# Attention of an adaLN block: one add of the softmax sum moved from VectorE to TensorE

## The reference

```python
scores = jnp.einsum('bhqd,bhkd->bhqk', q, k) / math.sqrt(hd)
causal = jnp.tril(jnp.ones((l, l), bool))
scores = jnp.where(causal, scores, -jnp.inf)
att = jax.nn.softmax(scores, axis=-1)
out = jnp.einsum('bhqk,bhkd->bhqd', att, v)
out = out.transpose(0, 2, 1, 3).reshape(b, l, d)
return out @ Wo.T + bo
```

## Time and profile before

| what | value |
|---|---|
| median of 3 timed runs | 2920.46 us (2919.89 to 2921.38) |
| profiled execution | 2918.9 us |
| its span, first to last instruction | 2917.2 us |
| TensorE busy (matmuls) | 2764.7 us, 95% |
| VectorE busy | 1578.7 us, 54% |
| ScalarE busy | 1058.9 us, 36% |
| GpSimd busy | 1281.3 us, 44% |
| mean granted TensorE clock | 0.979 of full speed |

### The profile page before, as it was taken

One profiled execution on the slowest core, in us unless ns is written; L12 is line 12 of the kernel. 1 busy time (PEld: TensorE's weight loads), 2 busy tenths in 40 slices (PEclk: granted clock), 3 DMA queues, 4 the chain that ended last, 5 costly groups with the idle time before them and its releaser, 6 DMA issues. The chain is left out here.

```text
span 2917.2 us, 41697 instructions
## 1 busy us (share of the span) xinstructions
PE 2764.7 (95%) x16180; PEld 2009.6 (69%) x16180; DVE 1578.7 (54%) x3165; ACT 1058.9 (36%) x1446; POOL 1281.3 (44%) x672
## 2 busy tenths in 40 slices
PE   4999999999999999889999999999999958999997
PEld 2888888888888888645555555555555527888886
DVE  4232223222323122267887777777777726777775
ACT  1322322122113111245666656556565631112121
POOL 2322332242225111267777777777777741212120
PEclk8999999999999999899999999999999979999998
DMA  7444343334335644365555555555555244544541
GB/s 250 161 159 160 140 181 134 140 116 173 116 115 169 213 164 168 127 138 121 117 117 118 122 127 127 118 126 127 128 121 117 67 146 142 148 148 138 166 130 58
DMA packets 153996, 404.85 MB, mean 139 GB/s; under 512 B 21820, under 2 KB 57076, under 8 KB 152776
## 3 DMA queue, kind: packets, MB, share of 16 engines
q1 hardware_dynamic: 123480, 292.05, 29.4%
q10 hardware_dynamic: 30320, 110.15, 17.7%
HBM read 270.41 MB, written 131.20 MB: 138 GB/s over the span
## 5 line engine op out<-in xcount | busy, mean ns | idle before, releaser
L1093 ACT ACTIVATE prob<-ps_s 128x1024 f32<-128x1024 f32 (+3 forms) x768 | 597.2, 810 | 407.2 <-PE ps_s L1231 390.4
L787 PE MATMUL ps_u<-h_hi,w_hi 128*128 128x512 f32 x1536 | 612.5, 399 | 2.0 <-POOL h_lo L555 2.0
L787 PE MATMUL ps_u<-h_lo,w_hi 128*128 128x512 f32 x1536 | 601.3, 391 | 0.0
L787 PE MATMUL ps_u<-h_hi,w_lo 128*128 128x512 f32 x1536 | 600.0, 391 | 0.0
L1049 POOL TENSOR_TENSOR added<-added,prob 128x2048 f32<-128x2048 f32 (+1 forms) x128 | 550.5, 4301 | 4.6
L549 POOL TENSOR_TENSOR w_lo<-w_raw,w_hi 128x1024 fp32r<-128x1024 f32 x93 | 222.6, 2393 | 473.1 <-ACT w_hi L617 473.1
L678 DVE SCALAR_TENSOR_TENSOR qk_lo<-ps_u,bias_col,qk_hi 128x512 fp32r<-128x512 f32 x128 | 96.0, 750 | 578.9 <-ACT qk_hi L593 578.9
L1135 DVE TENSOR_REDUCE part_high<-ps_r 128x1 f32<-128x512 f32 x496 | 330.6, 686 | 88.1 <-PE ps_r L1201 88.1
L1131 DVE CUSTOM_DVE_ANT_0 ps_r<-ps_r,row_mask 128x384 f32<-128x384 f32 (+1 forms) x500 | 312.5, 630 | 108.7 <-PE ps_r L1201 107.6
L1201 PE MATMUL ps_r<-k_st,q_st 96*128 96x512 f32 (+1 forms) x1008 | 330.9, 386 | 16.8 <-DMA v_sb<-v_tok 9.0
L787 PEld LDWEIGHTS ps_u<-h_lo,w_hi 128*128 128x128 f32 x1536 | 288.7, 188 | 61.6
(11 more groups left out here) (197 smaller groups left out, 3429.6 us busy)
## 6 DMA issues: line engine op xcount, KB each, us to landing
w_raw<-w_cols SPq DMA_DIRECT2D x72, 512.0 KB, 6.2
qk_split<-qk_hi SPq DMA_DIRECT2D x64, 512.0 KB, 2.6
qk_split<-qk_lo SPq DMA_DIRECT2D x64, 512.0 KB, 4.1
q_st<-qk_split ACTq DMA_DIRECT2D x60, 512.0 KB, 7.5
k_st<-qk_split ACTq DMA_DIRECT2D x60, 512.0 KB, 13.6
xn<-in_L_attn_x SPq DMA_DIRECT2D x8, 2048.0 KB, 12.8
v_tok<-v_out SPq DMA_DIRECT2D x32, 512.0 KB, 4.4
wm<-in_L_wmod SPq DMA_DIRECT2D x8, 2048.0 KB, 8.0
```

Of the source, the lines that this page charges most:

```text
L787: last = nc.tensor.matmul(ps_u[u % 2][:], w[:, m, k], h[:, k, tok], start=k == 0 and j == 0, stop=k == KT - 1 and j == 2)
L1093: nc.scalar.activation(prob[:, buffer_of(t, k), 2 * pair:2 * pair + 2, off:], ps_s[pair][:, :, off:], ACT.Exp, scale=SCALE).then_inc(exp_d ...
```

## The change

VectorE's first add (tile 8 + tile 9) goes. low_total now holds only columns 256 to 511, and begins with tile 9: the first remaining add is tile 9 + tile 10 in columns 256 to 511, the second adds tile 11 in columns 384 to 511. They stay behind the rows 3 and 5. sum_low has three pieces in place of two: tile 8 in all 512 columns, low_total in columns 256 to 511, and tile 9 in columns 128 to 255. TensorE waits in front of them for the mask of tile 9 where it waited for that of tile 8.

```diff
-    LOW_ADDS = CT - 1
-    LOW_AT = (1, 3, 5)
+    LOW_ADDS = CT - 2
+    LOW_AT = (3, 5)
...
             def add_low(t, i):
 
-                k = LONG + 1 + i
+                k = LONG + 2 + i
                 if i == 0:
...
-                so_far = prob[:, buffer_of(t, LONG), :, cols] if i == 0 else low_total[:, :, cols]
+                so_far = prob[:, buffer_of(t, LONG + 1), :, cols] if i == 0 else low_total[:, :, cols]
...
                 use = ("sum", t, 0)
                 bank_free(use)
-                pe.wait_ge(masked, masked_upto(t, LONG))
+                pe.wait_ge(masked, masked_upto(t, LONG + 1))
                 pe.wait_ge(low_added, LOW_ADDS * (t + 1))
-                for total, cols in ((low_total[:], slice(P, BANK)), (prob[:, buffer_of(t, LONG)], slice(0, P))):
+                parts = ((prob[:, buffer_of(t, LONG)], slice(0, BANK)), (low_total[:], slice(2 * P, BANK)), (prob[:, buffer_of(t, LONG + 1)], slice(P, 2 * P)))
+                for n, (total, cols) in enumerate(parts):
                     for h in range(HG):
-                        last = nc.tensor.matmul(bank_of(use)[h * HD:(h + 1) * HD, cols], ones[:], total[:, h, cols], start=cols.start > 0, stop=cols.start == 0)
+                        last = nc.tensor.matmul(bank_of(use)[h * HD:(h + 1) * HD, cols], ones[:], total[:, h, cols], start=n == 0, stop=n == len(parts) - 1)
                 last.then_inc(sum_done, 1)
```

## The result

The changed kernel takes **2951.04 us**, the median of 4 runs (2947.46 to 2954.66), where the kernel before took 2920.61 (2919.89 to 2921.38) beside it. The ratio is 1.0104, with a 95% interval of 1.0087 to 1.0122. It is slower, as forecast, but by 30.4 us where 19.8 were forecast, and 2951.0 lies above the range of 2929 to 2945.

What follows compares the result with a forecast made beforehand. TensorE's matmul order was taken to set the pace. 31 sums x 0.64 = 19.8 us, with no gain from VectorE, on the profiled 2918.9 plus 1.6 to the median gave 2940.3 us; range 2929 to 2945 us.

Steps and rivals of the forecast that it cites:

- Part 1: Lower half's sum on TensorE: three pieces take 1.64 us in place of 1.01, so 0.64 us more a group.
- Part 2: VectorE's removed first add, 1.75 us in each of 32 groups: TensorE gains 0 us from it.
- Part 3: The two remaining adds, masks, exponentials, copy and DMAs around the sum: they stay or shift with it, no further cost.
- Part 4: TensorE's 0.33 us idle in front of the lower sum is its own and stays: 0 us, at most 10.0 in all.
- Part 5: End of the stage: the second last sum's 0.64 us is absorbed by a wait for GpSimd's masks; the last sum counts.
- more than its length: Rival: the later sum makes a copy or exponential late, TensorE waits 0.33 us more a group: 30 us, 2951 us; 4%.
- VectorE was the pace: Rival: TensorE waits for VectorE, so 1.75 us comes off each group and 0.64 goes on: -34 us, 2886 us; 7%.
- half and half: Rival: the 0.33 us in front of the sum is VectorE's and goes: +9.8 us, 2930 us; 5%.
- TensorE has room: Rival: the lower half's longer sum grows into gaps on TensorE, no change: 2920 us; 5%.
- the rule on weight loads: Skill page's advice to read weight loads' busy share, 56% here, not matmul busy time; by it TensorE would have headroom.

Runs made afterwards that it cites:

- the two kernels with the loads taken apart: Changed kernel and kernel before, each with ScalarE's seven loads issued two behind steps 3, 4 and 5, one behind 6: 2930.69 and 2911.32 us.
- VectorE's part alone: Kernel before with VectorE's two adds as changed, TensorE's sum in its old shapes, so low_total is left out of it: 2918.84 us, ratio 0.9999.
- TensorE's part alone: Changed kernel with TensorE's three-piece sum, but VectorE still making three adds: 2950.54 us, ratio 1.0103 to the kernel before.
- the one with free increments: Changed kernel plus 120 semaphore increments in front of two early waits where TensorE is idle anyway: 2934.93 us, ratio 1.0047 to the kernel before.
- the split one: Kernel before with the lower sum's 128-column piece made as two of 64: 2928.91 us; with 120 increments in TensorE's early idle time 2915.22 us.
- one issue a step: Kernel before with ScalarE's seven loads of a round issued one each behind steps 4 to 10: 2924.68 us, ratio 1.0025.

## Why the prediction was wrong

- **Part 1, right.** 0.65 us a group at the sum, forecast 0.64; the two kernels with the loads taken apart differ by 19.4 us over the 31 sums that count, forecast 19.8.
- **Part 2, right.** The add was worth 0 us, by the kernel that has VectorE's part alone and by the one that has TensorE's.
- **Part 3 is the step that failed.** "their scores are issued by TensorE behind the sum too, so they shift with it and no further" and "No DMA is added or moved". I counted the added instructions as time on TensorE, and as nothing else. They are also a stream that is fetched, and 16 more in a round of 495 tuned the round to two blocks. A DMA was moved: the fetch, from 8 rounds' issues into all 29. In each of them it stretches ScalarE's second issue, and the exponentials of step 5, which stand behind the seven issues on ScalarE's queue, come late; TensorE waits for them before it makes the next scores. Its step from a row to the scores there, at 15 us of the round, takes 0.29 us on average before and 0.57 after, and the two steps behind it 0.13 us more together; 0.1 us comes back at 30 us, where the wait for the shift's loads is shorter.
- **Part 4, right.** 10.0 us in 30 groups, before and after. In the last group, with no row left for VectorE, it is still 0.34 us (the changed kernel's timeline, against the last row):

```profile
2392.09 1.06 PE L1266 MATMUL ps_r<-prob,ones 128*32 128x512 f32 x8 [0.34 <-PE ps_o L1251]
```

- **Part 5, right.** From the second last upper sum to the last it is 28.50 us before and 28.49 after: the longer sum between them was absorbed. In the last group the granted clock is 0.50 from 2354.9 to 2361.7 us before and from 2383.6 to 2390.4 us after, so times behind the last upper sum don't compare to better than some 0.5 us.

The sum, by what was measured: 31 x 0.65 = 20.2 us, and the collision. The changed kernel and the one with free increments differ by 16.1 us. In their profiled executions, 16.3 us apart, 13.5 us lie between the first and the last upper sum (1106.2 against 1092.7), 1.8 us in front and 1.0 behind; whether those 2.8 belong to the collision no run says. 13.5 us over 29 rounds are 0.47 us each, and before had 8 of them. An estimate for this stretch is 30 x 0.65 = 19.5, and 21 x 0.47 = 9.8 more, less 1.1 us for TensorE's waits for the shift's loads, which the longer round has ended. That makes 28.2; measured were 28.5. With the last sum it is 28.9 of the 30.4 us; the other 1.5 us stay unassigned.

Of the rivals, *more than its length* named the time, 2951 us, and half of the mechanism: an exponential is late and TensorE waits a second time. Its cause was wrong, since the sum's own length makes nothing late, and its price of 0.33 us was taken from another wait. At 4% it was no forecast. *VectorE was the pace* and *half and half* fall with the kernel that has VectorE's part alone. *TensorE has room* falls too, and with it the rule on weight loads: their share stayed at 56% (601.20 of 1080.00 us) while every added matmul counted.

The page Runtime: NRT & Kernel Launch of the Trainium skill (section "Instruction fetch mechanics") says that instructions come in blocks of 256, and that crossing a block costs something "mostly hidden". The block's size agrees, 2 packets more for 512 instructions. "Mostly hidden" the runs contradict where a row of DMA issues lies beside the fetch: moving the fetches away from it gave back 16.1 us in the changed kernel and 13.7 in the split one. TensorE itself isn't held up by the fetch; its steps that grew are the ones behind step 5's exponentials.

What stays open is which part of the chip the fetch and the issue share. The runs show that they meet in time, that a second issue is stretched beyond 0.74 us only when they do, and that an issue that stands alone isn't; nothing was tried that would name the shared part. Open too is how much of the price comes through the clock in single executions: the profiled one of the kernel with TensorE's part alone has two falls to 0.50, at 1443 and 1552 us, each behind a wait of more than 1 us for an exponential, and that of the changed kernel has none between 1300 and 2300 us.

## What to carry to other kernels

Where a loop is written out, count the instructions of its engine per round; near a multiple of the fetch block (511 against 2 x 256 here) the fetches stand still, and every round has the same collision or none. When a small edit costs more than its length, look in the DMA view at the instruction queue beside the longest row of DMA issues, and move the stream once by a few free instructions before blaming the edit. Don't put many DMA issues in a row in front of work that another engine waits for; take them apart, though not later than their data allow.

## What the runs showed of the hardware

- A fetch of TensorE's instructions that falls on the start of ScalarE's row of DMA issues stretches the next issue from 0.45 us to between 0.85 and 1.75 us (changed kernel; 0.70 to 1.47 in the split one). A fetch of another queue, q14, in the same place made it 0.50 to 0.74. An issue that stood alone beside a q8 fetch took 0.31 us, in 26 rounds.
- An issue of these 512 KB loads holds ScalarE's queue for 0.31 us (the first of a row) or 0.45 us (the fifth of the seven up to 0.77), and seven in a row for 3.5 us.
- Behind waits of 0.86 to 0.97 us of TensorE the granted clock fell three times from 1.00 to 0.50 for 3.4 us (one issue a step, kernel before); behind three others of 0.84 to 0.94 us it did not.
- A semaphore increment of its own takes some 0.15 us on TensorE (one starts every 0.151 us at the start of its program); 120 of them are free where TensorE waits for its inputs anyway, 256 at the start cost 24.8 us.
